# The normalisation step of six layer norms moved from VectorE to GpSimd in a two-layer decoder

## What is computed

```python
def _layernorm(x, axis=-1, eps=1e-05):
    m = jnp.mean(x, axis=axis, keepdims=True)
    v = jnp.var(x, axis=axis, keepdims=True)
    return (x - m) / jnp.sqrt(v + eps)
...
    x = x + _L0_attn_ref(_layernorm(x, axis=-1), ...)        # latent attention, 16 heads of 16
    x = x + _L0_xattn_ref(_layernorm(x, axis=-1), ctx_1024, ...)  # attention over the 16 heads of each token
    x = x + _L0_ffn_ref(_layernorm(x, axis=-1), ...)         # the best 128 tokens go through a GELU block
    x = x + _L1_attn_ref(_layernorm(x, axis=-1), ...)        # attention, only the 25 best scores of a row kept
    x = x + _L1_xattn_ref(_layernorm(x, axis=-1), ctx_1024, ..., _lenS2, ...)  # masked cross attention
    x = x + _L1_ffn_ref(_layernorm(x, axis=-1), ...)         # a ternary linear layer
```

## Time and profile before

| | us |
|---|---|
| median of 3 runs | 7603.36 |
| lowest, highest | 7600.09, 7605.11 |
| span of the profiled execution | 7598.9 |

### The profile page before, as it was taken

One profiled execution on the slowest core, in us unless ns is written; L12 is line 12 of the kernel. 1 busy time (PEld: TensorE's weight loads), 2 busy tenths in 40 slices (PEclk: granted clock), 3 DMA queues, 4 the chain that ended last, 5 costly groups with the idle time before them and its releaser, 6 DMA issues. The chain is left out here.

```text
span 7598.9 us, 125913 instructions
## 1 busy us (share of the span) xinstructions
PE 6235.0 (82%) x42626; PEld 4768.3 (63%) x42626; DVE 4669.9 (61%) x16147; ACT 4599.4 (61%) x11425; POOL 2259.9 (30%) x3108
## 2 busy tenths in 40 slices
PE   6788887888888888878888888888788888888876
PEld 5666666666666666666666666666666666666654
DVE  2665566655566655666555666556675556665555
ACT  4666565665666665656656666656566566665553
POOL 1322233322233222333222332223332223322222
PEclk8999999999999999999999999999999999999987
DMA  1000000000000000000000000000000000000000
GB/s 67 7 8 8 7 2 8 8 8 7 4 7 8 8 8 7 2 8 8 8 7 4 7 8 8 8 7 2 8 8 8 7 4 7 8 8 8 5 1 5
DMA packets 25717, 63.10 MB, mean 8 GB/s; under 512 B 3939, under 2 KB 5604, under 8 KB 23652
## 3 DMA queue, kind: packets, MB, share of 16 engines
q1 hardware_dynamic: 24932, 53.32, 2.6%
HBM read 44.92 MB, written 8.39 MB: 7 GB/s over the span
## 5 line engine op out<-in xcount | busy, mean ns | idle before, releaser
L420 DVE TENSOR_REDUCE b_nm<-bankB 128x2 f32<-128x512 f32 x512 | 354.0, 691 | 977.3 <-PE bankB L319 974.6
L992 DVE MATCH_REPLACE8 wk<-m,wk 128x256 f32<-128x256 f32 x2048 | 819.4, 406 | 0.0
L1048 POOL TENSOR_TENSOR b_pr<-b_pr,sc 128x512 f32<-128x512 f32 x512 | 654.4, 1278 | 512.7 <-ACT b_pr L919 512.7
L329 PE MATMUL bankB<-ident,b_pr 128*128 128x128 f32 x4096 | 681.1, 291 | 144.1 <-ACT b_pr L942 132.7
L988 DVE MAX8 m<-wk 128x8 f32<-128x256 f32 x2048 | 756.6, 410 | 0.0
L632 ACT ACTIVATE vT_qm<-bankA,xb 64x256 f32<-64x256 f32 x1024 | 481.2, 470 | 412.7 <-PE bankA L462 391.0
L337 ACT ACTIVATE b_pt<-bankB 128x512 f32<-128x512 f32 x1024 | 612.8, 598 | 188.2 <-PE bankB L329 188.0
L329 PEld LDWEIGHTS bankB<-ident,b_pr 128*128 128x128 f32 x4096 | 487.6, 146 | 352.8 <-ACT b_pr L942 204.6
L319 PE MATMUL bankB<-b_kq,b_qm 128*128 128x256 f32 x2048 | 653.1, 449 | 2.7 <-POOL b_qm L393 2.7
L420 DVE TENSOR_REDUCE a_nm<-bankA 128x2 f32<-128x512 f32 x512 | 351.9, 687 | 432.4 <-PE bankA L319 432.4
L413 ACT ACTIVATE b_pr<-bankB,b_nm 128x256 f32<-128x256 f32 x1024 | 429.9, 475 | 308.1 <-DVE b_nm L420 308.1
(11 more groups left out here) (199 smaller groups left out, 14097.8 us busy)
## 6 DMA issues: line engine op xcount, KB each, us to landing
xin<-x_in SPq DMA_DIRECT2D x32, 256.0 KB, 3.4
ctxA<-ctx_in SPq DMA_DIRECT2D x32, 256.0 KB, 2.7
ctxB<-ctx_in SPq DMA_DIRECT2D x32, 256.0 KB, 4.3
out<-x SPq DMA_DIRECT2D x32, 256.0 KB
xq_area<-w_groupq SPq DMA_DIRECT2D x32, 128.0 KB
vT_qm<-w_groupk SPq DMA_DIRECT2D x32, 128.0 KB
w<-w_w SPq DMA_DIRECT2D x2, 1024.0 KB
xwq<-w_xwq SPq DMA_DIRECT2D x1, 1024.0 KB
```

What stands on the lines that cost most here:

```text
L329: last = nc.tensor.transpose(bank[:, c * S + t * P:c * S + (t + 1) * P], b["pr"][:, h % 2, t, c * P:(c + 1) * P], w["ident"][:])
L420: nc.vector.tensor_reduce(b["nm"][:, h, :], bank[:].rearrange("p (t s) -> p t s", t=NT), AX.X, ALU.max, negate=True).then_inc(g[n + "_nm"], 1)
L992: m = nc.vector.match_replace(out=wk[:, k, t, :], in_to_replace=take, in_values=src[:, t, :], imm_value=-BIG)
L1048: nc.gpsimd.tensor_tensor(sp_[:, h % 2], taken[:, h % 2], sc[:, h % 3], ALU.mult).then_inc(g["sp_mul"], 1)
```

## The change

ln_dve2 becomes ln_pool2. The same two instructions for each layer norm, with the same operands and the same semaphores, are issued on GpSimd's queue, at once behind ln_pool's power, for all six layer norms. They are gone from VectorE's queue. Nothing else is moved, and the tables of places are the same.

```diff
-        def ln_dve2(dve, k, x, ln):
-            dve.wait_ge(g[f"ln{k}_rstd"], 1)
+        def ln_pool2(pool, k, x, ln):
+            pool.wait_ge(g[f"ln{k}_rstd"], 1)
             for t in range(NT):
-                nc.vector.tensor_scalar(ln["xn"][:, t, :], x[:, t, :], ln["mv"][:, t, 0:1], ln["rs"][:, t:t + 1],
+                nc.gpsimd.tensor_scalar(ln["xn"][:, t, :], x[:, t, :], ln["mv"][:, t, 0:1], ln["rs"][:, t:t + 1],
                                         ALU.subtract, ALU.mult).then_inc(g[f"ln{k}_xn"], 1)
...
                 ln_dve(dve, 1, x1, lnA, [])
                 yield A1 + 1.7
-                ln_dve2(dve, 1, x1, lnA)
...
                 ln_pool(pool, 1, lnA)
+                ln_pool2(pool, 1, x1, lnA)
                 yield A1 + 2.8
```

More of the change, by code:

```diff
@@ L750, in vector_a @@
                 yield A2 + QUADS + 2
-                ln_dve2(dve, 0, xin, lnM)
             if mode["mix"]:
@@ L758, in vector_a @@
                 yield A3 + 1.6
-                ln_dve2(dve, 2, x2, lnA)
                 yield A3 + 5.4
@@ L794, in vector_a @@
                 yield A3 + 8.9
-                ln_dve2(dve, 3, x3, lnA)
             if mode["mla"]:
@@ L827, in pool_a @@
                 ln_pool(pool, 0, lnM)
+                ln_pool2(pool, 0, xin, lnM)
             if mode["mix"]:
@@ L830, in pool_a @@
                 ln_pool(pool, 2, lnA)
+                ln_pool2(pool, 2, x2, lnA)
                 yield A3 + 2
@@ L842, in pool_a @@
                 ln_pool(pool, 3, lnA)
+                ln_pool2(pool, 3, x3, lnA)
         BS = H + 4
@@ L1010, in vector_b @@
             yield C0 + 1.9
-            ln_dve2(dve, 4, x4, lnB)
             for h in range(H):
@@ L1021, in vector_b @@
             yield L0 - 0.1
-            ln_dve2(dve, 5, x5, lnB)
             yield L0 + 1.5
@@ L1053, in pool_b @@
             ln_pool(pool, 4, lnB)
+            ln_pool2(pool, 4, x4, lnB)
             yield C0 + 2.5
@@ L1062, in pool_b @@
             ln_pool(pool, 5, lnB)
+            ln_pool2(pool, 5, x5, lnB)
             yield L0 + 1.1
```

## The result

The changed kernel is slower, by 0.6%. Its median is 7649.9 us (7646.6 to 7651.0) against 7601.7 (7598.1 to 7605.1) for the kernel before; the ratio is 1.0064, 95% interval 1.0049 to 1.0078. The prediction was 7451 in a range of 7405 to 7545. The profiled execution spans 7649.2 us where the one before spanned 7598.9.

The account below looks back on a forecast made before the run. No engine is full; stretches of a pass have different limits. Gains of 5.5 us in 20 long and 4.1 in 11 short passes, less 2.5 elsewhere, make 152: 7598.9 - 152 + 4.5 = 7451 us, range 7405 to 7545.

Parts of the forecast that it names:

- ln1: Start of a pass: TensorE's wait for this normalisation goes, gaining 1.65 us in long passes, 0.3 in short ones.
- ln0: Inside the sort: VectorE saves 0.66 us of a saturated stretch, making the sum 2.31 long, 0.96 short.
- ln2: End of the sort: VectorE skips wait and normalisation, gaining 1.77 us; its scores become last only above about 2 us a pair.
- The price of the pair: Two normalisation instructions on GpSimd: 0.62 us each, 1.26 in all with the semaphore wait, against VectorE's 0.73 + 0.04.
- naked pair: Normalisation directly on the deciding path, at ln4 and ln5: +0.49 us each, 0.98 us lost a pass.
- the bound of +1.8: High end of the moved pair's extra cost, a whole 512-element product of 1.28 us for each instruction: 7570.
- After the selection TensorE is busy nearly throughout, so nothing else eats or returns the shift.: From selection to pass end: only 0.98 us lost at ln4 and ln5, leaving 5.5 us long, 4.1 short.
- The rival on TensorE's clock: From ln1's transposes to the first maximum, a lower clock takes back 1.35 us a long pass: 7478; chance 0.10.
- The relief in the selection: Mixture-of-depths routing: rank starts before GpSimd's masks, so the chain takes 4.08 us instead of 6.46, gaining 2.38.
- dear pair: Slower rival: the moved instructions cost more on GpSimd; gain gone at about 1.5 us each, near 7720 at 2.0; chance 0.06.
- hold VectorE's sort up: Rival: GpSimd's pair slows the sort by 1.19 us at ln0 and at ln2, 74 us less gain: 7525; chance 0.06.
- Relief missing: Rival at the selection: masks come forward as far as the rank, so 74 us less gain: 7525; chance 0.14.

Follow-up runs that it names:

- the form with shorter waits: Changed kernel with one difference and one product of a full and a broadcast operand over both token tiles, instead of two two-operation instructions: 7675.3 us, ratio 1.0103.

## Why the prediction was wrong

Its first half held. ln1 gave 1.27 us at the first maximum (1.17 forecast), ln0 brought it to 1.93 at the sum ahead of ln2 (1.83 forecast). The selection lost its collision with the masks and TensorE its wait. x3 came 5.39 us earlier, where 5.98 were forecast; that this is close is luck, since steps 3 and 4 below missed in opposite directions. The steps that failed:

1. **The price of the pair.** I took 0.62 us an instruction, on the argument that it streams one full operand. It takes 1.22. The naked pair costs +1.78 us instead of +0.49; at ln4 and ln5 that is 3.56 instead of 0.98 a pass, 80 us over 31 passes. The size was inside the bound of +1.8 that the prediction set, by which the time would have been 7570, already outside its stated range. What was wrong was which row stands for it. Of the 0.61 us between the broadcast product (0.61) and the moved form (1.23), half is there with a single operation of the tensor-scalar kind (0.92), the other half is the second operation (0.31); the number of streamed operands doesn't give the order, as the difference of two full tensors takes 0.72.
2. **"After the selection TensorE is busy nearly throughout, so nothing else eats or returns the shift."** The dear price at ln4 and ln5 makes 7451 + 80 = 7531, still inside the range, and with the 0.6 us missing at x3 it is 7550, at its edge; this step brings it to 7645, and 7650 was measured. 3.07 us a pass, 95 us in all, went into matmuls at the lower clock, before ln4's sum and behind ln4 and ln5. The waits were priced by their length, with no term for the clock behind them. The rival on TensorE's clock looked for it at ln1, where nothing was given back, and the sum's later terms had none. Idle transposes in the waits for ln4 and ln5 brought 52 to 67 us back by the medians (58 to 68 by the ratios) with the pair's price left as it was. The 1.09 us ahead of ln4's sum stand behind no moved pair: the kernel before with the masks held loses 1.32 there, so an earlier selection alone is enough for them.
3. **ln2.** The rank was to start 3.60 us earlier and started 1.75 earlier, since VectorE had the sort done and then waited 4.55 us for scores that came through ln2's pair, a wait of TensorE of 2.60 us and a projection at the lower clock. The prediction named this turn for a pair over 2 us, but held the pair for shorter.
4. **The relief in the selection** was mis-sized the other way, 2.38 us instead of 3.70 (the chain's mean before is 6.21, 6.46 in 20 of the 29 passes and 5.64 in 9). I split the chain into a part ahead of the masks and the last two comparisons; but the masks at 2443.18 had run beside all but the first 0.8 of the 6.46 us. The undisturbed chain of the earlier trace rows, 2.51 us as a whole, was the number to take; it came out as 2.50. This and 1.08 us of faster matmuls from the selection matmul to x3, where TensorE no longer comes out of a wait of 4.23 (mean clock 1.00 instead of 0.87), are why step 3 hardly shows at x3.

Of the rivals, "dear pair" was right in kind. Its break-even of 1.5 us an instruction is refuted, though: at 1.22 the change already loses, because of point 2. GpSimd's pair didn't hold VectorE's sort up: a head's first search takes 387 to 429 ns in the changed kernel, 385 to 429 before. "Relief missing" is refuted for this kernel, and true for the one with ln2 on VectorE.

The sum, again by pass: forecast -5.0, plus 0.6 up to x3, plus 2.58 for the price, plus 3.07 for the clock gives +1.25, where the table has +1.31 at x1 (the shift of 0.07 between x3 and the first scores makes the difference). Outside the 31 passes the change costs more than the 2.5 us forecast: the launch's second pass alone, which runs ln1, ln0, ln2 and ln3 without the sort beside them, takes 153.7 us instead of 147.1.

What stays open: what lets the clock fall in one pass and not in the next. The projection behind ln4 took from 1.99 to 3.78 us in the kernel before, too, the clock ahead of ln4's sum fell behind a wait that had not changed, and the form with shorter waits had the slower linear layer. The runs show that filling a wait mends the matmuls right behind it, and no more than that.

## What to carry to other kernels

Before a step is moved to an engine with time to spare, find the places where it is naked, and price them twice: the longer wait, and the matmuls behind it at the upper and at the lower level of the clock, since nothing here told beforehand which it would be. Do the same for the waits that only shift. Take the price from a row with the same kind of instruction, number of operations and operands, and where there is none, believe the dear end of the bound. And when a gain comes from two engines no longer meeting, look for the wait that parts them directly; here one wait did it, for 103 us.

## What the runs showed of the hardware that I had not expected

- Work added to TensorE's waits makes the kernel faster: 28 idle transposes a pass (3.4 us) gained 52 us, 48 (5.6 us) 67 us in the changed kernel, 12 in a wait of 2.91 us 42 us in another (by the medians).
- A wait of the same 2.10 us leaves the projection behind it at the upper level in 29 of 29 passes of one kernel and in 1 and 2 of two others.
- On GpSimd one instruction with two operations and two operands per partition on 256 columns takes 1.23 us, more than two products of the broadcast kind on the same columns (2 x 0.61).
- GpSimd's masks stretch VectorE's comparison of one full operand, 0.47 us for two alone, to 2.04, more than four times, while they are hardly slower themselves (8.57 us for eight beside the chain, 8.03 behind it), and they leave the searches of the sort alone.
